# Two graph-convolution layers and a slot FFN: unchecked gathers with zero rows, lists gathered at any edge, x in ring slots, waits per copy in the tail

## The reference, cut to what matters

```
def gcn_conv(x, edge_index, W, b, n_nodes):     # edge_index gets one more loop per node
    deg = segment_sum(ones, dst);  dinv = where(deg > 0, rsqrt(deg), 0)
    h = x @ W.T
    return segment_sum(h[src] * (dinv[src] * dinv[dst])[:, None], dst) + b
x = x + gcn_conv(relu(gcn_conv(layernorm(x), W1, b1)), W2, b2)
Xn = l2_normalize(layernorm(x));  logits = Xn @ (l2_normalize(slot_params) * scale)     # 32 slots
Dw = softmax(logits, over nodes);  C = softmax(logits, over the 32 slots)
Y = gelu((Dw.T @ Xn) @ W_down + b_down) @ W_up + b_up       # 8 experts, 4 slots, 96 hidden
out = x + C @ Y
```

## Time and profile before

| | |
|---|---|
| median of 3 runs | 2862.25 us (2860.14 to 2864.53) |
| profiled execution | 2881.27 us, span 2879.6 us, mean granted TensorE clock 0.867 |
| busy | PE 2127.8, DVE 1723.6, GpSimd 1683.2, PE weight loads 1309.1, ACT 531.5 us |
| DMA | 834.62 MB, mean 290 GB/s |
| start | to the loop's first gather at 221.89 us |
| layers | 2 x 49 tiles, to about 2697 us |
| tail | the rest |

### The profile page before, as it was taken

How to read it: one execution, slowest core, us unless ns; L and a number is a source line. 1 busy time by engine, 2 the same in 40 slices (tenths; PEclk the granted TensorE clock), 3 DMA queues, 4 the chain that set the end, 5 groups by cost and what they waited for, 6 DMA issues and landing times.

```text
span 2879.6 us, 27437 instructions
## 1 busy us (share of the span) xinstructions
PE 2127.8 (74%) x7723; PEld 1309.1 (45%) x7724; DVE 1723.6 (60%) x2263; ACT 531.5 (18%) x985; POOL 1683.2 (58%) x1752
## 2 busy tenths in 40 slices
PE   6615777777777777777766777778777777887768
PEld 6603444444444444444434444445444444454534
DVE  8654666655666665566645666565566656655536
ACT  7840101101111010111101111111111111111220
POOL 3246666666666666666656666666666666666300
PEclk9997898888888888988878888898888888888969
DMA  9497888888888888888868988888888888888766
GB/s 339 158 380 270 278 283 290 285 282 294 281 290 282 291 287 286 299 279 284 291 242 280 329 299 302 298 311 299 302 301 299 299 308 314 298 296 324 286 216 262
DMA packets 228816, 834.62 MB, mean 290 GB/s; under 512 B 61676, under 2 KB 62460, under 8 KB 228748
## 3 DMA queue, kind: packets, MB, share of 16 engines
q0 software_dynamic: 135968, 633.20, 63.1%
q1 hardware_dynamic: 64964, 158.63, 15.3%
q10 hardware_dynamic: 27836, 42.21, 4.0%
HBM read 784.81 MB, written 81.21 MB: 301 GB/s over the span
## 4 chain that ended last, share of the span: by engine, by line
PE 36%; issue 23%; DVE 12%; DMA 9%; POOL 9%; another core or an unknown queue 6%; ACT 3%; DVEq 1%; POOLq 0%; SPq 0%; ACTq 0%
PE work L1411 15%; PE left L1440 13%; DVE acc L1159 8%; DMA rows<-table_layer,gidx 7%; POOL rows L684 5%; POOL rows L691 3%; PE fixed L1398 2%; PE work L1426 2%; ACT logits L756 1%; ACT xsT L745 1%; PE fixed L1387 1%; DVE hot L1117 1%; PE acc L1547 1%; PE fixed L1547 1%
## 5 line engine op out<-in xcount | busy, mean ns | idle before, releaser
L1159 DVE TENSOR_TENSOR acc<-acc,rows 128x768 f32<-128x768 f32 x1078 | 1038.6, 963 | 761.5 <-DMA rows<-table_layer,gidx 534.7
L684 POOL DMA_INDIRECT rows<-table_layer,gidx x1176 | 1114.3, 948 | 359.9 <-issue 357.2
L1411 PE MATMUL work<-WT,aggT 128*128 128x384 f32 x2352 | 883.6, 538 | 250.4 <-issue 142.0
L1440 PE MATMUL left<-rows,hot 128*128 128x384 f32 x1960 | 826.7, 553 | 237.5 <-issue 235.3
L1411 PEld LDWEIGHTS work<-WT,aggT 128*128 128x128 f32 x2352 | 496.1, 213 | 642.7 <-issue 278.7
L691 POOL DMA_INDIRECT rows<-table_layer,gidx x490 | 490.4, 1001 | 484.9 <-remote 216.7
L1440 PEld LDWEIGHTS left<-rows,hot 128*128 128x128 f32 x1960 | 396.6, 214 | 512.4 <-issue 369.1
L847 ACT ACTIVATE aggT<-fixed 128x768 f32<-128x768 f32 x98 | 79.4, 810 | 1040.1 <-remote 1020.8
L815 ACT ACTIVATE acc<-rows 128x768 f32<-128x768 f32 x98 | 79.8, 815 | 822.2 <-DMA rows<-table_layer,gidx 641.6
L1398 PE MATMUL fixed<-ident,xs 128*128 128x128 f32 x294 | 68.8, 401 | 91.0 <-issue 78.0
L1398 PEld LDWEIGHTS fixed<-ident,xs 128*128 128x128 f32 x294 | 55.7, 213 | 128.1 <-issue 112.8
(11 more groups left out here) (323 smaller groups left out, 1321.1 us busy)
## 6 DMA issues: line engine op xcount, KB each, us to landing
self_row<-table_layer SPq DMA_DIRECT2D x98, 384.0 KB
rows<-table_layer,gidx POOLq DMA_INDIRECT x1666
xstage<-in_x SPq DMA_DIRECT2D x67, 384.0 KB
xs<-in_x SPq DMA_DIRECT2D x58, 384.0 KB
table_layer<-ynext SPq DMA_DIRECT2D x48, 384.0 KB
xnew<-xs SPq DMA_DIRECT2D x47, 384.0 KB
table_layer<-xstage ACTq DMA_DIRECT2D x40, 384.0 KB
rows<-xnew SPq DMA_DIRECT2D x18, 384.0 KB
```

The source lines that it names most:

```text
L684: pool.indirect_dma_start(rows[:, slot, :], None, table[l][0:ROWS, :], bass.IndirectOffsetOnAxis(ap=gidx[:, k % 2, slot:slot + 1], axis=0) ...
L1159: dve.tensor_tensor(acc[:, :, 0:H], acc[:, :, 0:H], halves(row), ALU.add).then_inc(S["added"], 1)
L1411: m = pe.matmul(work[:, h, 0:H], aggT[:, kc, :], WT[l][:, kc, h * H:(h + 1) * H], start=kc == 0, stop=kc == KC - 1)
L1440: m = pe.matmul(left[:, h, 0:H], hot[:, b, c, :], rows[:, slot, h * H:(h + 1) * H], start=c == 0, stop=c == LEFT - 1)
```

## The change

1. The left-over gathers have no bounds check, and an empty left-over place gets the index of the partition's row of zeros in place of one beyond the table.
2. `src_windows` is now the edge list itself, seen as rows of one element, and a gather of 40 edges starts at the node's first edge. ACT's DMA, the shift of the index and the nine shift operations per part are gone; the parts have 17, 16, 10 and 6 tiles.
3. Eleven loads of x for the y table go to slots 7 to 17 of `rows`, as soon as the degree counting has read what lay there.
4. DVE takes the squares of the slots' norms ahead of the degrees, the variances and their roots ahead of the window indices, and the table's factors right behind them.
5. In the tail, W_up comes on a lane of its own, which only the up matmuls wait for; the biases' matmuls stand ahead of the wait for gelu; the token softmax (ACT's exponential and DVE's normalisation) stands later; the accumulators change places; the first y matmuls wait for the number of `y_slots` copies that they read; the last output tile is stored as 96 and 10 rows, each on a lane of its own.

```diff
-REACH = 48
-STEP = 8
-ANCHORS = -(-(E // STEP + 1) // P) * P
+REACH = OWN + EXTRA
+RING_X, RING_X0 = 11, 7
-WINDOW_PARTS = ((0, 13), (13, 25), (25, 37), (37, T))
+WINDOW_PARTS = ((0, 17), (17, 33), (33, 43), (43, T))
+EVEN = LAST // 16 * 16
-        src_windows = dram("src_windows", [ANCHORS, REACH], i32)
+        src_windows = src_pad[0:E + REACH].rearrange("(n o) -> n o", o=1)
...
             # x_buf(n), load_x(n)
+            if T <= n < T + RING_X:
+                return rows[:, RING_X0 + n - T, :]
+        def before_in_buf(n):
+            return n - XBUFS if n >= T + RING_X + XBUFS else n - XBUFS - RING_X
...
-                if n >= T:
-                    m = n - XBUFS - RELOADED
+                if n == T:
+                    sp.wait_ge(s["onehots_used"], GROUPS)
+                if n >= T + RING_X:
+                    m = before_in_buf(n) - RELOADED
                     sp.wait_ge(y_out[m % X_LANES], 16 * (m // X_LANES + 1))
...
             # load_tail, and what calls it; out_load(t) is one higher
+                if n == LOADED:
+                    sp.dma_start(wup, a["W_up"].rearrange("n h d -> h n d")).then_inc(fx_in[n % 4], 16)
+                    return
...
-            sp.dma_start(wup, a["W_up"].rearrange("n h d -> h n d")).then_inc(F["w_in"], 16)
+            load_tail(LOADED)
...
             for b in range(4):
-                sp.wait_ge(f_out[b], done_count(b, 4))
+                sp.wait_ge(f_out[b], 16 * len(range(b, T + 1, 4)))
...
             # GpSimd
-            last_anchor = pool.to_reg(ANCHORS - 1)
-            pool.wait_ge(s["windows_out"], 16)
+            last_edge = pool.to_reg(E)
+            pool.wait_ge(s["pads_in"], 64)
             pool.wait_ge(s["window_idx_ready"], 1)
...
-                    pool.indirect_dma_start(windows_i[:, t, :], None, src_windows[:, :],
-                                            bass.IndirectOffsetOnAxis(ap=anchor[:, t:t + 1], axis=0),
-                                            bounds_check=last_anchor, oob_is_err=False).then_inc(landed, 16)
+                    pool.indirect_dma_start(windows_i[:, t, :], None, src_windows,
+                                            bass.IndirectOffsetOnAxis(ap=node_first[:, t:t + 1], axis=0),
+                                            bounds_check=last_edge, oob_is_err=False).then_inc(landed, 16)
...
                             rows[:, slot, :], None, table[l][0:ROWS, :],
-                            bass.IndirectOffsetOnAxis(ap=gidx[:, k % 2, slot:slot + 1], axis=0),
-                            bounds_check=bound, oob_is_err=False).then_inc(rows_in[slot], 16)
+                            bass.IndirectOffsetOnAxis(ap=gidx[:, k % 2, slot:slot + 1], axis=0)
+                            ).then_inc(rows_in[slot], 16)
...
             # ACT
-            act.wait_ge(s["pads_in"], 64)
-            act.dma_start(src_windows[:, :].rearrange("(p n) w -> p n w", p=P),
-                          bass.AP(src_pad.tensor, 0, [[STEP * ANCHORS // P, P], [STEP, ANCHORS // P], [1, REACH]])
-                          ).then_inc(s["windows_out"], 16)
...
-                if t == THIRDS[1][1]:
-                    act.wait_ge(F["exp_in"], len(THIRDS) + 1)
-                    act.activation(cw[:, :, :], cw[:, :, :], ACT.Exp).then_inc(F["exp_done"], 1)
+            act.wait_ge(F["exp_in"], len(THIRDS) + 1)
+            act.activation(cw[:, :, :], cw[:, :, :], ACT.Exp).then_inc(F["exp_done"], 1)
...
-                n = LAST if t == T - 1 else P
                 act.wait_ge(F["out_ready"], t + 1)
-                if t >= 4:
-                    act.wait_ge(f_out[t % 4], 16 * (t // 4))
-                act.dma_start(a["out"][t * P:t * P + n, :], out_buf(t)[0:n, :]).then_inc(f_out[t % 4], 16)
+                for n, (r0, r1) in enumerate(((0, EVEN), (EVEN, LAST)) if t == T - 1 else ((0, P),), t):
+                    if n >= 4:
+                        act.wait_ge(f_out[n % 4], 16 * (n // 4))
+                    act.dma_start(a["out"][t * P + r0:t * P + r1, :], out_buf(t)[r0:r1, :]).then_inc(f_out[n % 4], 16)
...
             # DVE: the norms' squares and the variances with roots_in move ahead, as in point 4
             def window_indices():
                 dve.wait_ge(s["sums_out"], 2)
                 one.then(dve.tensor_copy(node_first, node_starts))
-                one.then(dve.tensor_scalar(anchor, node_first, 3, None, ALU.arith_shift_right))
                 dve.sem_inc(s["window_idx_ready"], 1)
+                dve.wait_ge(s["roots_out"], 3)
+                one.mark(dve.tensor_copy(dinv[:, :], recip_deg))
+                one.then(dve.tensor_tensor(coef, recip_var[:, 0:T], recip_deg[:, 0:T], ALU.mult))
+                one.then(dve.tensor_tensor(shift, nmean[:, :], coef, ALU.mult))
+                dve.sem_inc(s["coef_ready"], 1)
...
-            for bit in range(3):
-                one.then(dve.tensor_scalar(bit_i, node_first, bit, 1, ALU.arith_shift_right, ALU.bitwise_and))
-                one.then(dve.tensor_copy(bits[bit], bit_i))
...
-                    dve.tensor_scalar(groups(pick_col[:, 2, :]), found[:, :, :, 0], 0.0, FAR, ALU.is_equal, ALU.mult
+                    dve.tensor_scalar(groups(pick_col[:, 2, :]), found[:, :, :, 0], 0.0, zero_row[:, 0:1], ALU.is_equal, ALU.mult
...
                 one.then(dve.tensor_copy(win, windows_i[:, t0:t1, :]))
-                for bit in (2, 1, 0):
-                    far = 1 << bit
-                    n = OWN + EXTRA + far - 1
-                    moved = moved_all[:, :, 0:n]
-                    one.then(dve.tensor_tensor(moved, win[:, :, far:far + n], win[:, :, 0:n], ALU.subtract))
-                    one.then(dve.tensor_tensor(moved, moved, bits[bit][:, t0:t1].unsqueeze(2).to_broadcast([P, nt, n]),
-                                               ALU.mult))
-                    one.then(dve.tensor_tensor(win[:, :, 0:n], win[:, :, 0:n], moved, ALU.add))
...
             # PE
-            pe.wait_ge(F["w_in"], 16 * (EXPERTS + 3))
+            pe.wait_ge(F["w_in"], 16 * (EXPERTS + 2))
...
+            for h in range(2):
+                pe.matmul(fixed[strip_of(0), h, 0:H], sel[:, 0, :], bup[:, h * H:(h + 1) * H], start=True, stop=False)
+            pe.wait_ge(fx_in[LOADED % 4], 16 * (LOADED // 4 + 1))
             pe.wait_ge(F["gelu_done"], 1)
             for h in range(2):
-                pe.matmul(fixed[strip_of(0), h, 0:H], sel[:, 0, :], bup[:, h * H:(h + 1) * H], start=True, stop=False)
...
-            pe.wait_ge(F["y_slots_ready"], 4)
...
+                    if t < 3:
+                        pe.wait_ge(F["y_slots_ready"], t + 1 if t < 2 else 4)
```

More of the change, by code:

```diff
@@ L355, in x_buf @@
                 return parked[n - RELOADED]
-            return xbuf[(n if n < RELOADED else n - PARKED) % XBUFS]
+            if T <= n < T + RING_X:
+                return rows[:, RING_X0 + n - T, :]
+            return xbuf[(n if n < RELOADED else n - PARKED if n < T else n - PARKED - RING_X) % XBUFS]
+        def before_in_buf(n):
+            return n - XBUFS if n >= T + RING_X + XBUFS else n - XBUFS - RING_X
         wide_ec = EC + 2
@@ L400, in build @@
         eff_deg, extra, opens = scratch[:, 0:T], scratch[:, 64:64 + T], scratch[:, 512:512 + T]
-        node_first, anchor, bit_i = (scratch[:, c:c + T].bitcast(i32) for c in (128, 192, 256))
-        bits = [scratch[:, c:c + T] for c in (320, 384, 448)]
+        node_first = scratch[:, 128:128 + T].bitcast(i32)
         wide = T * REACH
@@ L411, in build @@
         sums_row, unsorted = acc[0:1, 0, 0:3 * TC], acc[0:1, 0, 3 * TC:3 * TC + 1]
-        accs = [acc, fixed, left]
+        accs = [fixed, left, acc]
         def logits_ps(t):
@@ L457, in out_load @@
         def out_load(t):
-            return LOADED + AGAIN.index(t)
+            return LOADED + 1 + AGAIN.index(t)
         block = ctx.enter_context(nc.Block())
@@ L602, in _ @@
             sp.wait_ge(F["mixed_done"], AHEAD + EXPERTS)
-            sp.dma_start(wup, a["W_up"].rearrange("n h d -> h n d")).then_inc(F["w_in"], 16)
+            load_tail(LOADED)
             sp.wait_ge(F["down_done"], 1)
-            for n in range(LOADED, LOADED + KC):
+            for n in range(LOADED + 1, LOADED + 1 + KC):
                 load_tail(n)
             sp.wait_ge(F["up_done"], 1)
-            for n in range(LOADED + KC, LOADED + len(AGAIN)):
+            for n in range(LOADED + 1 + KC, LOADED + 1 + len(AGAIN)):
                 load_tail(n)
             for b in range(4):
-                sp.wait_ge(f_out[b], done_count(b, 4))
+                sp.wait_ge(f_out[b], 16 * len(range(b, T + 1, 4)))
         @block.gpsimd
@@ L947, in _ @@
             dve.wait_ge(s["misc_in"], 64)
+            one.then(dve.tensor_tensor(aggT[:, :, 0:SLOTS], sp_c[:, :, :], sp_c[:, :, :], ALU.mult))
+            one.mark(dve.tensor_reduce(norm2_kq, aggT[:, :, 0:SLOTS].rearrange("p k (n q) -> p k q n", n=EXPERTS),
+                                       AX.X, ALU.add))
```

(24 more changed lines are left out.)

8 lines of the change are left out of this document (4 added, 4 removed).

## The result

The changed kernel takes 2839.37 us (median of four, 2832.55 to 2840.57) and the one before, beside it, 2861.19. The ratio is 0.9919, 95% interval 0.9899 to 0.9938: 23 us faster by the ratio (22 between the medians), where the forecast had 54 and the rival B, "the loop doesn't follow its train", 29. The time lies in the range given for 8 in 10 (2785 to 2850), at B's end of it. The forecast's sign was right and its size was not.

The account below looks back on a forecast made before the run. No engine fills the kernel; each loop tile was taken as its gathers in a row plus the last one's landing. Gathers 26 + start 16 + tail 13 = 55 us off 2862, forecast 2808; 8 in 10: 2785 to 2850.

Parts of the forecast that it names:

- rival B: Layer loop: GpSimd's wait takes up what the shorter gathers give, only start and tail gain; 2833 us, chance 0.20.
- the train plus the landing of its last member: Layer loop: a tile lasts its 17 gathers in a row plus the last own gather's landing, 25.05 us.
- The term of 26 us: Layer loop: five left-over gathers a tile without the check save 0.27 us, x 98 tiles; bounds 0 and 26.
- A left-over gather without the check is 53 ns faster: Layer loop: a gather takes 1001 ns with the check and 948 without, the whole difference given to the check.
- I carry the 19 over unchanged: Whole kernel: the profiled execution took 2881.3 us, 19.0 above the median of 2862.25; this offset was kept.
- Zero rows at no cost: Layer loop: 93 empty places a tile now read rows, 0.286 MB more, taken as 0 us; upper bound 1.00 a tile.
- The start, 16 us: Start: the loop's first gather at 205 to 207 in place of 221.9; bounds 22 us and a loss of 2.
- ACT's wait for W: Start: ACT waits 4.62 us for W's first load beside the removed copy; 2 to 3 us were expected back.
- 16.5 at best: Start, y stage: begins 5 us sooner and eleven early loads take 11.5 us off the full DMA stretch.
- The tail, 13 us: Tail: 4.3 + 0.6 - 0.4 + 3.0 + 5.8 = 13.3 us saved, bounds 6 and 16.
- W_up's wait: Tail: the fold matmuls no longer wait for W_up but only for their other input, 4.3 us back.
- Rival D: Layer loop: PE's release is tied to checked gathers; up to 340 us less, some 2480, chance 0.03.

Follow-up runs that it names:

- bytes alone: The kernel before with the check kept and zero rows read in empty left-over places: 1.0042 on a fast chip, 1.0001 on a slow one.
- gathers alone: The kernel before with unchecked left-over gathers and zero rows in empty places only: 0.9964 on a fast chip, 1.0029 on a slow one.
- all but the gathers: The kernel after with the left-over gathers' check and the index beyond the table put back: 0.9886 on a fast chip, 0.9896 on a slow one.
- half rows: The kernel before with each gather taking half a row, used twice, as many gathers, wrong sums: 0.9950 to before, on a fast chip.
- sixteen gathers: The kernel before without the fifth left-over gather of a tile, wrong sums: 0.9634 to before, on a fast chip.
- a longer train: The kernel before with the bounds check on the twelve own gathers of a tile too: 1.0193 to before, on a fast chip.

## Why the prediction was wrong, step by step

**The period is "the train plus the landing of its last member": wrong, and this is the step that failed.** It was inferred from a release that coincides with the last landing. On slow chip 3 a tile's gathers took 0.35 us less without the check, and waits took it, behind the train in layer 1 and within it in layer 2; the tile stayed at 25.1 us (medians in layers 1 and 2: 25.04 and 25.14 without the check, 25.07 and 25.13 before). The term of 26 us was worth -8 in the measured time. By the packets in the traces the last own gather still landed 3.2 us behind the end of its issue, with the check and without; in layer 1 the next tile then started 0.8 us behind that landing in place of 0.6. So the landing coincides with the release and doesn't set it alone. I had named "nobody knows what holds PE's release" as what speaks for rival B, and yet gave it 0.20. That the period is the same in both layers fits a train, but it fits everything else that goes with the gathers as well.

**"A left-over gather without the check is 53 ns faster": right**, with 56 ns on chip 3 (1001 and 945) and 62 on a fast one (1011 and 949). On fast chips most of it is paid out: between bytes alone (1.0042) and gathers alone (0.9964) lies 0.78%, 20 us, where the term had 26.

**"I carry the 19 over unchanged": a wrong reading without effect on the sum.** Such an offset was no cost of profiling. More costly would have been to subtract the two profiles: 2881.3 - 2832.6 = 48.7 us looks like a confirmed forecast. Their tiles differ by 0.2 us, but the tile on chip 3 is 25.1 us with or without the check, and 98 times 0.2 is the 20 us by which the kernel before itself differs between the two chips (2861 and 2881). So most of this 0.2 is one chip against another; no trace of before from the first measurement's chip exists to show it.

**Zero rows at no cost: right on the slow chip, wrong on fast ones**, where the slack of the queue is 3 to 6% and one burst of other loads uses it up.

**The start, 16 us: 14 measured** (207.5 against 221.9, and 208.0 against 221.9 for all but the gathers on chip 3). That it came so close is in part luck. ACT's wait for W didn't shrink at all: 4.62 us in both the earlier trace rows, the copy beside it was no cause. So the y stage started at 123.31 and not at 120.5. It ended (last activation) at 199.5 against 210.1, 10.6 us sooner where the forecast had 16.5 at best. The lists were handed on at 200.98, 15 us sooner than the earlier trace rows, where the forecast had 198. Its own step from there doesn't come out either: 198 and 6 us are 204, not 205 to 207; measured were 6.5 us from 201.0.

**The tail, 13 us: 15 to 18 measured.** W_up's wait went as said, the store's end took the 3.3 us forecast, and the y matmuls start 24.1 us behind the folds (2761.50 - 2737.36) in place of 28.3, 4.1 us sooner where my terms had 3.2.

Sum on a slow chip: 30 from the ends, -8 from the gathers, 22 us; 22 to 23 were measured. The ends' 29 came out as a sum of terms that were each some us off, and rival B's 2833, which is 6 us below the measured time, priced the gathers at nothing where they cost 8. Rival D's "some 2480" doesn't follow from its own terms: 2862 - 340 - 29 = 2493. It had no effect on the forecast.

**Open.** What sets 25.1 us on a slow chip. It follows neither 0.35 us less of issue a tile nor 0.29 MB more. A fixed time per gather (25.1 / 17 = 1.48 us) or something that holds PE would both fit; half rows, sixteen gathers and a longer train would have told, but ran on a fast chip. Open too is where the 8 us of the unchecked gathers arise. In the profile they are spread, 2 to 3 us each in layer 1, between the layers, in layer 2 and behind it, but all but the gathers, with every check in place, also shows 2 us more in layer 1 than the first profile, so that these parts can't be told from noise.

## What to carry to other kernels

A term that rests on a wait whose releaser one can't explain is not a term: price it at both ends and let the lower one count fully. Before two profiles are subtracted, compare a stretch that the change doesn't touch, or run one of them again; a chip can differ by more than the change. And where a change adds bytes to a loop, look for the loop's one burst of other transfers, not at its mean load.

## What the hardware showed that was not expected

The same program takes 2547 us on four chips and 2881 on a fifth, 13% more, steadily. A gather takes as long on either (948 and 951 ns) and so does an addition of DVE (963 ns in both); what differs is when engines go on. Timeline of DVE and PE in the start of the kernel before, first the profile of the earlier trace rows, then that on a fast chip:

```profile
178.12 2.18 PE L1353 MATMUL work<-xsT,before_end 128*128 128x30 f32 x10
...
193.09 0.16 DVE L1048 TENSOR_TENSOR pick_col<-slot_of,work 128x6 f32<-128x6 f32 x1 [14.21 <-remote]
```

```profile
172.47 2.17 PE L1353 MATMUL work<-xsT,before_end 128*128 128x30 f32 x10
...
174.75 0.16 DVE L1048 TENSOR_TENSOR pick_col<-slot_of,work 128x6 f32<-128x6 f32 x1 [1.52 <-PE work L1353]
```

PE's matmuls end, by the record, at 180.3 and at 174.6; DVE, which waits for nothing else, goes on 12.8 us later on the slow chip and 0.1 us later on the fast one. GpSimd issues its gathers in both. On the slow chips DVE was let go at 192.5 to 193.1 in all six profiles, whether PE had ended at 176.8 or at 183.1, and 4 to 5 us behind the end of the last window gather, as in the loop behind the last own one. In the loop PE itself stands still in that time. Timeline of PE in the tile of the earlier trace rows:

```profile
744.39 0.48 PE L1440 MATMUL left<-rows,hot 128*128 128x384 f32 x1 [1.18 <-issue]
746.49 4.45 PE L1440 MATMUL left<-rows,hot 128*128 128x384 f32 x9 [1.62 <-issue]
```

It goes on at 746.49, with no releaser that the profile shows (over all tiles its left sums have 235.3 us of such idle before them, and on the fast chip 24.3 us of idle of any kind), and DVE follows at 746.66, ACT at 746.79 and GpSimd at 747.48. PE and those that wait for it, held until a train of gathers has landed, are thus the mark of the slow kind. The cause is not shown: whether the lower granted clock (0.867 against 0.905) is part of it or comes from the waits was not tested.
